# Graph layer on one core: comparison tables cut into pieces on VectorE, and two jobs moved to ScalarE

## The chip, the core and the metric

The kernel runs on one core of one Trainium2 chip. The metric is the device time of one execution in microseconds (us). Five engines work beside each other and meet only at semaphores: TensorE (PE, with its weight loads as PEld), VectorE (DVE), ScalarE (ACT), GpSimd (POOL) and SyncE (SP, which issues DMAs).

## What is computed

12,500 nodes with 256 features go through a layer norm, and then three things are added to them: a relational graph convolution over 200,000 edges of 8 types (per node and type the mean of the weighted neighbours, times that type's matrix), a linear attention with 8 heads over all nodes, and, after a second layer norm, a mixture of 6 expert networks of which the best 2 count for each node. Cut to its core:

```python
def gnn(x, src, dst, etype, ew, weight, root, bias):
    seg = etype * N + dst
    sums = segment_sum(x[src] * ew[:, None], seg)
    h = sums / maximum(segment_sum(ones, seg), 1)[:, None]        # mean by (type, dst)
    return einsum('rnc,rco->no', h.reshape(R, N, C), weight) + x @ root + bias

def mix(x):                                                       # 8 heads of 32
    q, k = elu(x @ wq + bq) + 1, elu(x @ wk + bk) + 1
    out = (q @ (k.T @ v)) / (q @ k.sum(rows) + 1e-6)              # by head
    return out @ wo + bo

def ffn(f):
    p = softmax(relu(f @ rw1 + b1) @ rw2 + b2); w, i = top_k(p, 2)
    h1 = relu(f @ e_w1[e] + e_b1[e]); h2 = relu(h1 @ e_w2[e] + e_b2[e])
    return sum over the two best e of softmax(w) * (h2 @ e_w3[e] + e_b3[e])

xn = layernorm(x)
x = x + gnn(xn, ...) + mix(xn)
return x + ffn(layernorm(x))
```

## The kernel before

**Two halves.** The first (up to about 610 us) normalizes the nodes, multiplies each by the 8 type matrices into a table `y_tab` in HBM, and builds for each edge a triple in `etab`: row of `y_tab`, target node, coefficient. The second half first makes the keys' sums of the attention (about 615 to 860 us) and then loops over 24 full super-tiles of 512 nodes (4 tiles of 128) and a last one of 2 tiles. One turn of that loop is `iteration(i, plan)`; there is one on each engine, and the engines keep step by semaphores alone. Nothing reorders instructions: each engine runs its own list as written.

**What one iteration does.** For super-tile `i` it runs the experts, and for the next one, `i+1`, it sums the edges and the attention. The edges of a super-tile come in 12 portions `p` of 6, 6 and 5 columns for each tile, a column being 128 edges. GpSimd gathers their rows from `y_tab` into `ring`. A 0/1 table of 128 edges by 128 nodes (one where the edge's target is the node) turns the sum over edges into a matmul, `aggregate(n, p)` on PE, into the PSUM tile `acc`. Portions 0 to 3 (`PLAIN`) are "weighted": VectorE writes coefficient times table into `sel` (`weighted`, L1376) and PE multiplies `ring` as it is. Portions 4 to 11 are "split": ScalarE writes the high half of coefficient times row (`high`, `row_hi`), VectorE the rest (`low_rows`, `row_lo`) and the bare 0/1 table `hot_r` (`one_hot`, L1386), one instruction for the whole portion; PE multiplies both halves.

**What a table is made of.** `iota_w` (SBUF) and `ramp` (its copy in PSUM) hold 0 to 127 along each row. `rel_w[:, n % 2, t, k]` is the target node of column `k` less the tile's first node; `tables(n)` makes it for a super-tile from the loaded triples `tab`. Comparing the one with the other gives the table.

**Where a portion is prepared and used.** With expert `e` VectorE and ScalarE prepare the portions of `SPLIT_AT[e]`, and PE sums those of `AHEAD_W3[e]`:

```python
AHEAD_W3 = {0: (3,), 1: (4,), 2: (5, 6), 3: (7, 8), 4: (9, 10), 5: (11,)}
SPLIT_AT = {0: (4,), 1: (5, 6), 2: (7, 8), 3: (9, 10), 4: (11,)}
```

So portions 5 and 6 are prepared with expert 1 and summed with expert 2, between PE's `h1` of expert 3 and its `w3` of expert 2. Portions 0 and 1 of `i+2` are prepared at the very end of iteration `i`.

**PE's banks.** Five PSUM banks are dealt out in turn to all results (`layout`), each freed by the engine that read it last. Per expert these are two results `h2(e)`, two `h1(e+1)` and two `w3(e)` (two tiles each). ScalarE and VectorE together take the hidden ones (`h_hi`, then `h_lo` on VectorE); VectorE alone takes `w3`: the instruction at L1552 adds bank times gate to `y`, twice for each bank. `queries` opens an iteration with two banks of query projections.

**The attention's denominators** (expert 1): VectorE adds epsilon, takes the reciprocal `rden` (128 x 32) and spreads it over the features into `rden_c`, which is the tile `eq` (128 x 1024); PE transposes that later (`spread`, expert 2).

## Time and profile before

| | |
|---|---|
| median of 3 runs | 2996.17 us (2993.83 to 2996.44) |
| the profiled execution | 2996.88 us, of which the span of its instructions is 2995.4 us |
| busy in the span | PE 2914.0 us (97%), VectorE 2190.0 us (73%), ScalarE 1762.9 us (59%), GpSimd 1674.2 us (56%) |
| mean granted TensorE clock | 0.991 |
| one iteration of the loop | 87.6 us (start to start of `std_c` on ScalarE: 1470.62 and 1558.22 us) |

Busy means that an instruction of the engine was in flight. An engine starts the next instruction a little before the one ahead has ended, so the time from start to start is shorter than a duration: twelve `sel` of 342 ns (median) took 3.16 us together.

### The profile page before, as it was taken

The numbers are of one execution on the slowest core, as the hardware profiler recorded it, in microseconds if no ns is written. First come the engines' busy times: TensorE is split into PE (matmuls) and PEld (weight loads), VectorE is DVE, ScalarE is ACT, GpSimd is POOL, SyncE is SP. The second block draws the span as 40 slices with busy tenths as digits, with TensorE's granted clock in tenths as the row PEclk, the third lists the DMA queues.
The fourth block names the chain that finished last, engine by engine and source line by source line (L and its number), as shares of the span: only waits on it lengthen the run. The fifth ranks groups of instructions, "written<-read, shape, count | busy, mean of one in ns | idle before, by whom it ended". The sixth has DMA issues, their size and how long they took to land.

```text
span 2995.4 us, 47258 instructions
## 1 busy us (share of the span) xinstructions
PE 2914.0 (97%) x16707; PEld 2561.0 (85%) x16708; DVE 2190.0 (73%) x5317; ACT 1762.9 (59%) x3392; POOL 1674.2 (56%) x1700
## 2 busy tenths in 40 slices
PE   7999999979989999999999999999999999999998
PEld 5887878868878888888888988888988888888887
DVE  5489564145677887777788777778887777888775
ACT  4455555524456666665666666566665666666554
POOL 1000000052267777777777777777777777777750
PEclk9999999989999999999999999999999999999999
DMA  7777777765444434444443444444344444434430
GB/s 275 272 264 274 265 275 288 293 214 199 145 130 127 128 109 133 134 130 134 122 130 106 129 130 132 133 122 126 114 134 134 134 124 130 121 121 134 134 85 11
DMA packets 181936, 471.35 MB, mean 157 GB/s; under 512 B 46902, under 2 KB 105228, under 8 KB 159715
## 3 DMA queue, kind: packets, MB, share of 16 engines
q0 software_dynamic: 80544, 221.54, 25.6%
q1 hardware_dynamic: 98960, 244.93, 22.6%
q8 instruction: 133, 2.18, 0.3%
q10 hardware_dynamic: 2196, 1.86, 0.2%
q14 instruction: 103, 0.84, 0.1%
HBM read 310.71 MB, written 158.29 MB: 157 GB/s over the span
## 4 chain that ended last, share of the span: by engine, by line
PE 63%; POOL 6%; DVE 5%; issue 3%; ACT 1%; DVEq 1%; DMA 0%; SPq 0%; ACTq 0%; POOLq 0%
PE bank L1670 41%; PE acc L1727 7%; PE acc L1733 7%; POOL ring L1150 6%; PE acc L1670 2%; DVE sel L1381 2%; PE bank L1834 1%; PE bank L1697 1%; DVE x L1480 1%; PE bank L1706 1%; PE bank L1716 1%; DVE h_lo L1510 1%; DVE stats_c L1484 1%; PE bank L1783 1%; DVEq L1482 1%
## 5 line engine op out<-in xcount | busy, mean ns | idle before, releaser
L1150 POOL DMA_INDIRECT ring<-y_tab,tab x1666 | 1657.5, 995 | 633.8 <-issue 499.7
L1224 ACT ACTIVATE h_hi<-bank,bias_t 128x512 fp32r<-128x512 f32 (+1 forms) x600 | 407.3, 679 | 302.1 <-PE bank L1670 268.5
L1510 DVE TENSOR_TENSOR h_lo<-bank,h_hi 128x512 fp32r<-128x512 f32 (+1 forms) x600 | 382.0, 674 | 229.8 <-ACT bank L1225 227.8
L778 PE MATMUL yb<-wr_hi,xhl 128*128 128x512 f32 x1568 | 498.2, 394 | 13.1 <-ACT yst L355 11.1
L1210 ACT ACTIVATE row_hi<-ring,tab 128x256 fp32r<-128x256 f32 x1091 | 451.7, 498 | 33.3 <-issue 17.7
L1401 DVE SCALAR_TENSOR_TENSOR row_lo<-ring,tab,row_hi 128x256 fp32r<-128x256 f32 x1091 | 449.4, 478 | 9.4 <-ACT row_hi L1210 9.2
L1225 ACT ACTIVATE bank<-bank,bias_t 128x512 f32<-128x512 f32 (+1 forms) x600 | 386.3, 644 | 0.0
L355 ACT ACTIVATE yst<-yb 128x512 f32<-128x512 f32 x392 | 229.3, 596 | 249.4 <-PE yb L778 219.1
L778 PEld LDWEIGHTS yb<-wr_hi,xhl 128*128 128x128 f32 x1568 | 296.2, 189 | 79.9 <-ACT yst L355 15.8
L1670 PE MATMUL bank<-ew_hi,h_hi 128*128 128x256 f32 x1176 | 343.5, 292 | 1.6 <-DVE h_lo L1510 1.4
L1670 PE MATMUL bank<-ew_lo,h_hi 128*128 128x256 f32 x1176 | 330.8, 281 | 0.0
L1670 PE MATMUL bank<-ew_hi,h_lo 128*128 128x256 f32 x1176 | 329.4, 280 | 0.0
L778 PE MATMUL yb<-wr_lo,xhl 128*128 128x512 f32 x784 | 306.9, 391 | 0.0
L1733 PE MATMUL acc<-row_hi,hot_r 128*128 128x256 f32 x1091 | 270.1, 286 | 10.7 <-DVE row_lo L1401 10.7
L1733 PE MATMUL acc<-row_lo,hot_r 128*128 128x256 f32 x1091 | 267.3, 283 | 0.0
L1727 PE MATMUL acc<-ring,sel 128*128 128x256 f32 x1150 | 264.4, 379 | 0.0
L1727 PEld LDWEIGHTS acc<-ring,sel 128*128 128x128 f32 x1150 | 214.2, 190 | 28.5
L1670 PE MATMUL bank<-h_hi,ew_hi 128*128 128x512 f32 (+1 forms) x600 | 236.7, 394 | 1.5 <-DVE h_lo L1510 1.5
L1552 DVE SCALAR_TENSOR_TENSOR y<-bank,gate,y 128x256 f32<-128x256 f32 x490 | 211.6, 477 | 35.4 <-PE bank L1670 28.9
L1670 PE MATMUL bank<-h_hi,ew_lo 128*128 128x512 f32 (+1 forms) x600 | 234.3, 390 | 0.0
L1670 PE MATMUL bank<-h_lo,ew_hi 128*128 128x512 f32 (+1 forms) x600 | 234.2, 390 | 0.0
L1670 PE MATMUL bank<-ft_hi,ew_hi 128*128 128x512 f32 (+1 forms) x600 | 232.9, 388 | 0.0
(265 smaller groups left out, 5506.6 us busy)
## 6 DMA issues: line engine op xcount, KB each, us to landing
y_tab<-yst SPq DMA_DIRECT2D x97, 1024.0 KB, 4.4
ring<-y_tab,tab POOLq DMA_INDIRECT x1666, 2.8
xt_tab<-xhl SPq DMA_DIRECT2D x25, 1024.0 KB, 4.8
xc<-xt_tab SPq DMA_DIRECT2D x25, 1024.0 KB, 5.5
xhl<-xt_tab SPq DMA_DIRECT2D x23, 1024.0 KB, 5.0
x<-x_tab SPq DMA_DIRECT2D x49, 256.0 KB, 3.1
xs<-in_x SPq DMA_DIRECT2D x24, 512.0 KB, 6.0
x_tab<-xs SPq DMA_DIRECT2D x24, 512.0 KB, 5.1
```

Source lines behind the costliest of these rows:

```text
L355: act.activation(yst[:, h, 2 * b:2 * b + 2, :], yb[(YB * u + b) % 3][:, :].rearrange("p (r n) -> p r n", r=2), ACT.Copy).then_inc(y_ev, 1)
L778: last = pe.matmul(out_ap, a, b, start=(i == 0), stop=(i == len(parts) - 1))
L1150: pool.indirect_dma_start(out=out_ap, out_offset=None, in_=y_tab[:, :], in_offset=bass.IndirectOffsetOnAxis(ap=idx_ap, axis=0)).then_inc(s ...
L1210: last = act.activation(row_hi[:, p % BUFS, q, :], ring[:, p % SLOTS, q, :], ACT.Copy, scale=tab[:, n % 2, t, k, 2:3])
L1224: act.activation(dest[:, m, 0:W], b[:, 0:W], ACT.Relu, bias=bias)
L1225: act.activation(b[:, 0:W], b[:, 0:W], ACT.Relu, bias=bias).then_inc(h_set, 1)
L1401: last = dve.scalar_tensor_tensor(out=row_lo[:, p % SLOTS, q, :], in0=ring[:, p % SLOTS, q, :], scalar=tab[:, n % 2, t, k, 2:3], in1=row_h ...
L1510: gone(dve.tensor_tensor(lo_[:, m, 0:W], bank[plan[kind, (e, m)][0]][:, 0:W], hi[:, m, 0:W].bitcast(F32), ALU.subtract))
L1552: last = dve.scalar_tensor_tensor(out=y[:, t, :], in0=b[:, (t % 2) * C:(t % 2 + 1) * C], scalar=gate[:, t, e:e + 1], in1=(y if e else x1)[ ...
L1670: last = pe.matmul(out_ap, a, b, start=(begin and i == 0), stop=(not more and i == len(parts) - 1), skip_group_check=more)
L1727: last = pe.matmul(sums(t), sel[:, p % BUFS, q, :], ring[:, p % SLOTS, q, :], start=False, stop=False, skip_group_check=True)
L1733: last = pe.matmul(sums(t), hot_r[:, p % BUFS, q, :], half, start=False, stop=False, skip_group_check=True)
```

## The change

- **Tables in pieces.** `split(n, p)` takes the place of `one_hot` and `low_rows` in the loop and in `prepare`: for each column one 128 x 128 piece of `hot_r`, then that column's `row_lo`. The wait for ScalarE's `hi_ready` stands ahead of the first piece. In an iteration the tables of a portion were made ahead of the expert's `y`; now they stand behind `y`, between the low rows. (The key stage keeps `one_hot` and `low_rows` for portions 4 to 7.)
- **`sel` from `ramp`.** `weighted` compares with `ramp` in PSUM where it read `iota_w` in SBUF.
- **`tables` on ScalarE.** Four activations for a super-tile, target node plus a bias column `neg_t` (a constant that GpSimd writes once), with expert 3; VectorE waits for `rel_set`. The first two super-tiles' are made at the head of the second half, ahead of all else on ScalarE's list.
- **The spread on ScalarE.** `by_feature` copies `rden` over the features, behind `gate_t` and ahead of the `row_hi` of portions 5 and 6; VectorE stops after the reciprocal.

```diff
+                def by_feature(i):
+                    act.wait_ge(rden_set, i + 2)
+                    act.activation(rden_c[:, :, :].rearrange("p t (h d) -> p (t h) d", h=HEADS),
+                                   rden[:, :, :].rearrange("p t h -> p (t h)").unsqueeze(2)
+                                   .to_broadcast([P, SUB * HEADS, C // HEADS]), ACT.Copy).then_inc(rden_ready, 1)
+                def tables(n):
+                    act.wait_ge(tab_in[n % 2], 16 * SUB * (n // 2 + 1))
+                    for t in range(SUB):
+                        last = act.activation(rel_w[:, n % 2, t, :], tab[:, n % 2, t, :, 1], ACT.Identity,
+                                              bias=neg_t[:, SUB * n + t:SUB * n + t + 1])
+                    last.then_inc(rel_set, 1)
...
+                        if more and e == 1:
+                            by_feature(i)
                         for p in SPLIT_AT.get(e, ()) if more else ():
                             high(i + 1, p)
+                        if more and e == EXPERTS - 3 and i + 2 < SUPER:
+                            tables(i + 2)
...
+                act.wait_ge(neg_set, 1)
+                tables(0)
+                tables(1)
...
-                    dve.reciprocal(rden[:, :, :], rden[:, :, :])
-                    dve.drain()
-                    dve.tensor_copy(rden_c[:, :, :].rearrange("p t (h d) -> p (t h) d", h=HEADS),
-                                    rden[:, :, :].rearrange("p t h -> p (t h)").unsqueeze(2)
-                                    .to_broadcast([P, SUB * HEADS, C // HEADS])).then_inc(rden_ready, 1)
+                    dve.reciprocal(rden[:, :, :], rden[:, :, :]).then_inc(rden_set, 1)
...
+                    dve.wait_ge(rel_set, n + 1)
                     tables_free(dve, n, p)
                     for q, (t, k) in enumerate(tiles_of_portion(p)):
-                        last = dve.tensor_scalar(sel[:, p % BUFS, q, :], iota_w[:, :], rel_w[:, n % 2, t, k:k + 1],
+                        last = dve.tensor_scalar(sel[:, p % BUFS, q, :], ramp[:, 0:NT], rel_w[:, n % 2, t, k:k + 1],
...
+                def split(n, p):
+                    if p >= parts(n):
+                        return
+                    tables_free(dve, n, p)
+                    if p == 0:
+                        dve.wait_ge(rel_set, n + 1)
+                    dve.wait_ge(hi_ready, split_before(n, p) + 1)
+                    for q, (t, k) in enumerate(tiles_of_portion(p)):
+                        dve.tensor_tensor(hot_r[:, p % BUFS, q:q + 1, :], ramp[:, 0:NT].unsqueeze(1).to_broadcast([P, 1, NT]),
+                                          rel_w[:, n % 2, t, k:k + 1].unsqueeze(2).to_broadcast([P, 1, NT]), ALU.is_equal)
+                        last = dve.scalar_tensor_tensor(out=row_lo[:, p % SLOTS, q, :], in0=ring[:, p % SLOTS, q, :],
+                                                        scalar=tab[:, n % 2, t, k, 2:3],
+                                                        in1=row_hi[:, p % BUFS, q, :].bitcast(F32),
+                                                        op0=ALU.mult, op1=ALU.subtract)
+                    last.then_inc(lo_ready, 1)
...
-                        for p in coming:
-                            one_hot(i + 1, p)
...
                             if h == 0 and coming:
-                                low_rows(i + 1, coming[0])
+                                split(i + 1, coming[0])
...
                         for p in coming[1:]:
-                            low_rows(i + 1, p)
-                        if more and e == EXPERTS - 3:
-                            if i + 2 < SUPER:
-                                tables(i + 2)
+                            split(i + 1, p)
```

VectorE with expert 3, where portions 9 and 10 are prepared. Before, from the hidden results' rest `h_lo` to the next expert's:

```order
L1390 TENSOR_TENSOR hot_r<-ramp,rel_w 128x768 [waits portion_used] x2
L1552 SCALAR_TENSOR_TENSOR y<-bank,gate,y 128x256 [waits items_full]
L1552 SCALAR_TENSOR_TENSOR y<-bank,gate,y 128x256
L1401 SCALAR_TENSOR_TENSOR row_lo<-ring,tab,row_hi 128x256 [waits hi_ready]
L1401 SCALAR_TENSOR_TENSOR row_lo<-ring,tab,row_hi 128x256 x5
L1372 TENSOR_SCALAR rel_w<-tab 128x17 [waits tab_in0]
L1372 TENSOR_SCALAR rel_w<-tab 128x17 x3
L1510 TENSOR_TENSOR h_lo<-bank,h_hi 128x512 [waits h_set] x4
```

The two `y` and the six `row_lo` stand there twice, once for each half of `w3`. After, the same stretch with one portion's pieces:

```order
L1578 SCALAR_TENSOR_TENSOR y<-bank,gate,y 128x256 [waits items_full]
L1578 SCALAR_TENSOR_TENSOR y<-bank,gate,y 128x256
L1429 TENSOR_TENSOR hot_r<-ramp,rel_w 128x128 [waits hi_ready,portion_used]
L1431 SCALAR_TENSOR_TENSOR row_lo<-ring,tab,row_hi 128x256
L1429 TENSOR_TENSOR hot_r<-ramp,rel_w 128x128
L1538 TENSOR_TENSOR h_lo<-bank,h_hi 128x512 [waits h_set] x4
```

The two tables of 768 columns that stood ahead of `y` have become twelve of 128 that stand behind it, each ahead of its low row, and the four `rel_w` are gone from this engine.

ScalarE with expert 1, between the gates' transpose `gate_t` and the high rows of portions 5 and 6. Before:

```order
L1250 ACTIVATE gate_t<-bank 96x512 [waits items_full]
L1210 ACTIVATE row_hi<-ring,tab 128x256 [waits portion_used,rows_in5,tab_in1]
L1210 ACTIVATE row_hi<-ring,tab 128x256 x4
L1210 ACTIVATE row_hi<-ring,tab 128x256 [waits portion_used,rows_in0,tab_in1]
L1210 ACTIVATE row_hi<-ring,tab 128x256 x5
```

After:

```order
L1266 ACTIVATE gate_t<-bank 96x512 [waits items_full]
L1205 ACTIVATE eq<-rden 128x1024 [waits rden_set]
L1226 ACTIVATE row_hi<-ring,tab 128x256 [waits portion_used,rows_in5,tab_in1]
L1226 ACTIVATE row_hi<-ring,tab 128x256 x4
L1226 ACTIVATE row_hi<-ring,tab 128x256 [waits portion_used,rows_in0,tab_in1]
```

The spread (`eq` is the tile under `rden_c`) now stands ahead of both portions' high rows.

## Rows read from the trace of the kernel before

**Rows 1.** Busy us (x instructions) by stretch: PE, PEld, DVE, ACT, POOL, clock, DMA.

```profile
1000.00:1900.00 900.00, 894.00 (x5450) 801.21 (x5449) 729.82 (x1903) 576.44 (x1095) 690.39 (x689) 1.00 0.43 126
```

**Rows 2.** Waits, PE's own: total us, times, longest.

```profile
PE bank L1670 <- DVE y L1552: 13.8, 23, 1.0
PE bank L1834 <- DVE kf_c L1584: 13.3, 5, 7.2
PE acc L1733 <- DVE row_lo L1401: 10.7, 4, 6.4
```

**Rows 3.** Timeline, VectorE, end of an iteration: start us, us, operation, xcount.

```profile
1464.09 3.16 DVE L1381 TENSOR_SCALAR sel<-iota_w,rel_w,tab 128x128 f32<-128x128 f32 x12
...
1470.68 1.66 DVE L1552 SCALAR_TENSOR_TENSOR y<-bank,gate,y 128x256 f32<-128x256 f32 x4
```

**Rows 4.** Timeline, PE, second query bank of the next iteration.

```profile
1471.61 0.72 PE L1670 MATMUL bank<-xc,wqr_hi 128*128 128x512 f32 x2 [0.57 <-DVE y L1552]
```

**Rows 5.** Groups by form, VectorE: busy us, mean ns of one, idle before.

```profile
L1401 DVE SCALAR_TENSOR_TENSOR row_lo<-ring,tab,row_hi 128x256 fp32r<-128x256 f32 x1091 | 449.4, 478 | 9.4 <-ACT row_hi L1210 9.2
...
L1552 DVE SCALAR_TENSOR_TENSOR y<-bank,gate,y 128x256 f32<-128x256 f32 x490 | 211.6, 477 | 35.4 <-PE bank L1670 28.9
L1381 DVE TENSOR_SCALAR sel<-iota_w,rel_w,tab 128x128 f32<-128x128 f32 x575 | 154.9, 356 | 78.5 <-PE acc L1727 78.4
L1390 DVE TENSOR_TENSOR hot_r<-ramp,rel_w 128x768 fp32r<-128x768 f32 x121 | 113.0, 950 | 2.2
...
L1390 DVE TENSOR_TENSOR hot_r<-ramp,rel_w 128x640 fp32r<-128x640 f32 x73 | 59.5, 815 | 0.0
...
L1495 DVE TENSOR_SCALAR xn_c<-x,mv_c,rstd_c 128x256 f32<-128x256 f32 x98 | 35.5, 422 | 2.0
...
L1359 DVE COPY eq<-rden 128x1024 f32<-128x1024 f32 x25 | 18.4, 734 | 1.8
```

**Rows 6.** Single lines, VectorE: copy into `ramp`, a table in SBUF (ns min/median/max).

```profile
L1304 DVE COPY ramp<-iota_w x1: 269/269/269, 605.9 to 605.9; 128x128 f32<-128x128 f32 x1
...
L513 DVE TENSOR_SCALAR place<-iota_w x1: 221/221/221, 175.0 to 175.0; 128x128 f32<-128x128 f32 x1
```

**Rows 7.** Groups by form, ScalarE.

```profile
L1228 ACT ACTIVATE std_c<-mv_c,eps_ln 128x4 f32<-128x4 f32 x24 | 7.1, 297 | 148.3 <-DVE mv_c L1487 148.3
...
L329 ACT ACTIVATE wr_hi<-yst 128x1024 fp32r<-128x1024 f32 x4 | 4.0, 1058 | 0.0
```

**Rows 8.** Timeline, ScalarE, expert 1 of an iteration.

```profile
1509.59 0.60 ACT L1250 ACTIVATE gate_t<-bank 96x512 fp32r<-96x512 f32 x1 [2.42 <-PE bank L1799]
1510.08 4.50 ACT L1210 ACTIVATE row_hi<-ring,tab 128x256 fp32r<-128x256 f32 x11
```

**Rows 9.** Timeline, VectorE, the same stretch.

```profile
1511.01 0.88 DVE L1552 SCALAR_TENSOR_TENSOR y<-bank,gate,y 128x256 f32<-128x256 f32 x2 [0.21 <-PE bank L1670]
1512.21 2.07 DVE L1401 SCALAR_TENSOR_TENSOR row_lo<-ring,tab,row_hi 128x256 fp32r<-128x256 f32 x5 [0.33 <-ACT row_hi L1210]
1514.20 0.87 DVE L1552 SCALAR_TENSOR_TENSOR y<-bank,gate,y 128x256 f32<-128x256 f32 x2
1515.16 1.29 DVE L1563 TENSOR_TENSOR y<-bank,y 128x512 f32<-128x512 f32 x2
1516.37 2.46 DVE L1401 SCALAR_TENSOR_TENSOR row_lo<-ring,tab,row_hi 128x256 fp32r<-128x256 f32 x6
```

**Rows 10.** Timeline, PE: first matmul of expert 3's `h1`; first of portion 6.

```profile
1515.49 0.39 PE L1670 MATMUL bank<-ft_hi,ew_hi 128*128 128x512 f32 x1
...
1519.43 0.28 PE L1733 MATMUL acc<-row_hi,hot_r 128*128 128x256 f32 x1
```

**Rows 11.** Timeline, VectorE, expert 3: first `y`, last low rows.

```profile
1534.68 0.88 DVE L1552 SCALAR_TENSOR_TENSOR y<-bank,gate,y 128x256 f32<-128x256 f32 x2
...
1538.63 2.46 DVE L1401 SCALAR_TENSOR_TENSOR row_lo<-ring,tab,row_hi 128x256 fp32r<-128x256 f32 x6
```

**Rows 12.** Timeline, PE, expert 3: last matmul of `w3`, half one; portion 10.

```profile
1534.05 0.28 PE L1670 MATMUL bank<-ew_hi,h_lo 128*128 128x256 f32 x1
...
1542.56 0.28 PE L1733 MATMUL acc<-row_hi,hot_r 128*128 128x256 f32 x1
```

More of the change, by code:

```diff
@@ L911, in gps_layer @@
             base_t = sbuf(pc, "base_t", [P, TILES_N])
+            neg_t = sbuf(pc, "neg_t", [P, TROWS])
             xtab = sbuf(pc, "xtab", [P, 3])
@@ L978, in gps_layer @@
             emptied = {"act": sem("act_emptied"), "dve": sem("dve_emptied")}
-            rden_ready, acc_full, x1_done = (sem(n) for n in ("rden_ready", "acc_full", "x1_done"))
+            rden_set, rel_set, rden_ready, acc_full, x1_done = (sem(n) for n in ("rden_set", "rel_set", "rden_ready", "acc_full", "x1_done"))
             var_c, std_c, xn_c, d_ready, ex_ready, gap_ready, g2_ready, gate_ready = (
@@ L996, in gps_layer @@
             rows_in = [sem(f"rows_in{g}") for g in range(SLOTS)]
-            xtab_in, xold_in, xrows_in, xrows_split, xsum_done, xnew_set, xnew_out, base_set, x_tab_done, xsum_free = (
+            xtab_in, xold_in, xrows_in, xrows_split, xsum_done, xnew_set, xnew_out, base_set, neg_set, x_tab_done, xsum_free = (
                 sem(n) for n in ("xtab_in", "xold_in", "xrows_in", "xrows_split", "xsum_done", "xnew_set", "xnew_out",
-                                 "base_set", "x_tab_done", "xsum_free"))
+                                 "base_set", "neg_set", "x_tab_done", "xsum_free"))
             def tiles(plan):
@@ L1143, in _ @@
                           allow_small_or_imprecise_dtypes=True).then_inc(base_set, 1)
+                pool.iota(neg_t[:, :], pattern=[[-NT, TROWS]], base=0, channel_multiplier=0,
+                          allow_small_or_imprecise_dtypes=True).then_inc(neg_set, 1)
                 def count(register):
@@ L1289, in _ @@
                         gone(act.activation(kw_sb[:, :, :], b[:, :].rearrange("p (k n) -> p k n", k=KC), ACT.Copy))
+                        by_feature(-1)
                     if p in WEIGHTS_AT:
@@ L1366, in attention @@
                         gone(dve.tensor_tensor(qf[:, k, :], qf[:, k, :], b[:, 0:NS], ALU.mult))
-                def tables(n):
-                    dve.wait_ge(tab_in[n % 2], 16 * SUB * (n // 2 + 1))
-                    for t in range(SUB):
-                        dve.tensor_scalar(rel_w[:, n % 2, t, :], tab[:, n % 2, t, :, 1], float(n * NS + t * NT), None,
-                                          ALU.subtract)
-                    dve.drain()
                 def weighted(n, p):
@@ L1411, in prepare @@
                     else:
-                        one_hot(n, p)
-                        low_rows(n, p)
+                        split(n, p)
                 def by_expert(v, n):
@@ L1596, in _ @@
                 dve.memset(zv[:, :, :, :], 1.0)
-                tables(0)
+                dve.drain()
                 for p in range(PARTS):
@@ L1627, in _ @@
                                           ALU.subtract).then_inc(w_split_c, 1)
-                tables(1)
                 prepare(1, 0)
```

## The prediction

> **What bounds the kernel now.** I read the busy time by stretch first. In the loop PE is busy 894.0 of 900 us, at full clock, while VectorE has 730 and ScalarE 576 [rows 1]. So work taken from VectorE or ScalarE buys nothing by itself. Time is won where PE waits, and lost where a later VectorE or ScalarE makes it wait. PE's own waits come next [rows 2]: in the loop one kind only, 23 times about 0.6 us for VectorE's `y`; the other two kinds belong to the key stage. The wait of 0.6 us stands at an iteration's start. VectorE runs twelve `sel`, then sums and statistics, without a pause into the four `y` [rows 3]; the second of these ends near 1471.55 us (half of 1.66 us after 1470.68), and PE's second query bank starts at 1471.61 [rows 4]. What stands in that row of VectorE is therefore paid or won one for one. Everywhere else the question is how long before PE's use VectorE is done.
>
> **Prices on VectorE.** Instructions start before the last one has ended: twelve `sel` in 3.16 us are 0.256 us from start to start, 0.09 less than the median duration of 0.342 us [rows 3]; five `row_lo` take the 1.99 us up to the next instruction, 0.398 each [rows 9]. I sum start-to-start times.
>
> *A piece of table.* 768 columns take 950 ns, 640 take 815 [rows 5]: 1.05 ns a column, 134 ns for 128. So 950 - 5 x 134 = 280 ns is a piece's duration and, less the same 0.08, 0.20 us its share. A column costs 0.20 + 0.40 = 0.60 us. A portion of 6 is 3.6 us behind `y` where it was 0.87 ahead and 2.38 behind; one of 5 is 3.0 where it was 0.73 and 1.99. Bounds: 0.13 if the fixed 0.07 is hidden beside a low row, 0.25 if alternating costs 0.05 more. I take 0.20, since both neighbours' rows give it.
>
> *`sel` from `ramp`.* No row shows this operation with PSUM as source. With two column scalars in SBUF the same operation costs (422 - 356)/128 = 0.52 ns a column, `hot_r` from `ramp` 1.05 [rows 5]. Bounds: nothing, or 128 x 0.53 = 0.07 us each. A gain is excluded as far as rows go: low rows from SBUF and `y` from PSUM take 478 and 477 ns [rows 5]. A copy of 128 x 128 into `ramp` took 269 ns, a table of that size in SBUF 221 [rows 6], which also speaks for the upper end. I take 0.07.
>
> The Trainium skill (VectorE: DVE Perf Modes, "Why PSUM operands drop a tier") says that the mode of two elements a cycle needs both read ports of SBUF, and that an fp32 operand in PSUM leaves one element a cycle. No run here shows a `sel` from PSUM. By that rule the upper end holds and the sum below stands; without it the first rival would.
>
> *Removed:* the spread (734 ns) and four small `rel_w`. The spread left a gap that VectorE spends waiting for PE at 1511.01 anyway [rows 9]; both count nothing.
>
> **ScalarE.** The spread is one activation of 128 x 1024; one of that size took 1058 ns [rows 7], 0.95 from start to start. Its wait is met: `rden` is ready before `gate_t`. What is queued behind it is `row_hi` of portions 5 and 6 [rows 8], and VectorE already waits 0.33 us for portion 5's [rows 9]. The four `rel_w` (297 ns for a small one with a bias column [rows 7], some 0.2 each) come with expert 3; all 0.8 us of them would only delay hidden results that VectorE reads behind portion 10's pieces, and their waiter, `sel`, comes two experts later. GpSimd's extra constant and the DMAs are off the path: no transfer is added.
>
> **The sum for one iteration,** place by place.
>
> 1. *End of the iteration.* 12 x 0.07 = 0.8 us more ahead of `y`, on the path already [rows 3, 4]: **+0.8**.
> 2. *Expert 1, bank.* Portion 5's high rows end 0.95 later, so the pieces start at 1513.17 and take 3.0: the second pair of `y` starts at 1516.16 where it started at 1514.20 [rows 9], and ends near 1517.04. PE needs that bank for expert 3's `h1`, which started at 1515.49 [rows 10]: **+1.6**.
> 3. *Portion 6.* Behind the `y` come 1.2 us of bias adds and 3.6 us of pieces: ready at about 1522.0. PE wanted it at 1519.43 [rows 10], now 1.6 later: 1521.0, **+1.0**.
> 4. *Portion 10.* With no tables ahead of it, VectorE's first `y` moves up to the end of PE's first half of `w3`, about 1534.4 [rows 12], instead of 1534.68 [rows 11]. Two pairs of `y` (0.8 each) and two portions (3.6 each) end at 1543.2; before it was 1541.1 [rows 11]. PE wants portion 10 at 1542.56 [rows 12]: **+0.7**.
>
> Portions 7 and 8 end about 1.2 later, portion 11 1.0; by the same sums they just arrive in time, and portion 4 easily does. Together 4.1 us. There are 23 iterations that prepare all 12 portions and a `sel` pair: 94 us. The 24th has expert 1's bank: 1.6. The head: about 17 `sel` of portions 1 to 3 and twelve ahead of the loop (29 x 0.07 = 2), VectorE's last four split portions back to back with the spread ahead of a `row_hi` (0.3 each and 0.95), and ScalarE's key work behind the loading of the second table (about 1.5): some 6, bounds 0 and 10. Sum: +101 us. The profiled execution took 2996.88 us with a span of 2995.4, so it lies 0.7 above the median, and the new time is 2996.9 + 101 = **3098 us**.
>
> **Rivals.**
>
> *First: `sel` costs the same from `ramp`.* For it: no row shows otherwise directly. Against it: the slopes [rows 5] and the copy into PSUM [rows 6]. Place 1 falls away (24 x 0.8 = 19) and 1 of the head: 3078 us.
>
> *Second: part of a piece is hidden.* The fixed 0.07 runs beside the low row, a column costs 0.53. Place 2 gives 1.3, place 3 0.6, place 4 none, place 1 stays: 2.7 x 23 + 1.3 + 5 = 68, thus 3065 us. Against it: no pair of operations in the rows overlaps more than 0.09.
>
> *Third: pieces dearer.* At 0.25 a piece places 2 to 4 are 1.9, 1.3 and 1.4, and portion 8 comes late by some 0.3: 5.7 x 23 + 9 = 140, thus 3137 us. For it: two more waits at the head of a portion, and operations change at every step.
>
> *Fourth, the other side: reading `ramp` runs beside reading SBUF.* A piece is then free beside its low row (a column 0.40), and `sel` falls to its 0.134 us of columns. VectorE would do the tables for nothing, place 1 turns to a gain of the whole 0.77 us that PE now loses there (24 x 0.77 = 18), places 3 and 4 vanish, and place 2 keeps 0.6 from the spread. That is -0.2 x 23 + 2 = about -3: 2994 us. It decides from a column of about 0.43 us and a `sel` under 0.19. Against it: `y`, which reads PSUM, and `row_lo` follow each other in the rows without any gain.
>
> **How the numbers follow.** Forecast 0.60, first rival 0.15, second 0.10, third 0.06, fourth 0.05, and 0.04 for a gain that I don't see. 0.2% (6 us) is about what a measurement of this kernel can tell from no change. The fourth lies within that, the unseen gain beyond it: faster 0.04, same 0.05, slower 0.91. The range reaches down past the second rival and its uncertain head to 3050, and up to the head's bound and pieces of 0.22, 3118; it leaves out the third, the fourth and the unseen gain, and some tails.
>
> **What would show it.** In the profile after: `hot_r` 1091 times at about 280 ns; `sel` at 410 ns instead of 342; an iteration of 91.7 us instead of 87.6; PE's wait for `y` at the query banks at 1.4 us; new waits of PE for `row_lo`, two in an iteration, and at expert 3's `h1` one for `y` of about 1.5; VectorE waiting 1.3 us for ScalarE's `row_hi` with expert 1. If the iteration is still 87.6 us, VectorE's prices are wrong; if `sel` stays at 342, the first rival holds; if `h1` doesn't wait with expert 1, the spread's place is.

## The result, and the profile after

The changed kernel takes 3107.82 us (median of 4 runs, 3106.42 to 3110.3) where the kernel before took 2995.0 us beside it (median of 4 runs, 2991.61 to 2996.44): 1.0379 times as long, 95% interval 1.0361 to 1.0397. That is 112.8 us more; the prediction was 101 more. The profiled executions differ by as much: a span of 3107.6 us against 2995.4.

Where the 112.2 us of span lie can be read from ScalarE's `std_c`, the square root that opens every turn of the loop. Its first instance starts at 869.28 us instead of 860.37: the head costs 8.9. From there to the last instance it is 103.6 us more, and the tail is 0.2 shorter. Two neighbours in the timeline of ScalarE after (start us, duration us, engine, line, operation; in brackets the idle time before it and who ended it):

```profile
1511.53 0.30 ACT L1244 ACTIVATE std_c<-mv_c,eps_ln 128x4 f32<-128x4 f32 x1 [6.61 <-DVE mv_c L1515]
...
1603.58 0.30 ACT L1244 ACTIVATE std_c<-mv_c,eps_ln 128x4 f32<-128x4 f32 x1 [6.61 <-DVE mv_c L1515]
```

A turn takes 92.05 us here and 92.02 in the middle of all, instead of 87.60: 4.42 more. The stretch of [rows 1] after, with the same columns:

```profile
1000.00:1900.00 900.00, 860.39 (x5178) 762.66 (x5178) 716.20 (x2114) 561.08 (x1086) 639.00 (x666) 1.00 0.41 122
```

PE's clock is at its upper level (1.00) as before, but PE is busy 860 of 900 us instead of 894: the time went into PE's waits, not into slower work of PE. VectorE is busy less than before (716 instead of 730) although it has 211 more instructions in these 900 us: fewer turns fit into them, and in each VectorE idles longer for PE, which waits for VectorE. The waits of PE in the whole execution, which answer [rows 2] (total us, times, longest us):

```profile
PE bank L1692 <- DVE y L1578: 65.0, 47, 1.4
PE acc L1755 <- DVE row_lo L1431: 38.8, 49, 6.7
PE bank L1856 <- DVE kf_c L1607: 20.1, 9, 12.5
```

The first kind had 23 waits, now 47: a second one in each turn. The second kind had 4, now 49: two new ones in each turn. The longest of the third, in the key stage, grew from 7.2 to 12.5 us; it belongs to the head.

The groups of VectorE by form, for [rows 5] (count | busy us, mean ns of one | idle before and its releaser):

```profile
L1431 DVE SCALAR_TENSOR_TENSOR row_lo<-ring,tab,row_hi 128x256 fp32r<-128x256 f32 x1068 | 506.7, 474 | 0.0
...
L1429 DVE TENSOR_TENSOR hot_r<-ramp,rel_w 128x128 fp32r<-128x128 f32 x1068 | 301.3, 282 | 35.7 <-ACT row_hi L1226 35.7
...
L1394 DVE TENSOR_SCALAR sel<-ramp,rel_w,tab 128x128 f32<-128x128 f32 x575 | 190.0, 402 | 81.9 <-PE acc L1749 81.9
```

A piece takes 282 ns and a `sel` from PSUM 402. There are 1068 pieces and not the 1091 that the prediction gave: the key stage keeps whole tables for portions 4 to 7, which are 23 columns. On ScalarE the spread takes 1044 ns and a small `rel_w` 303 (for [rows 7]):

```profile
L1205 ACT ACTIVATE eq<-rden 128x1024 f32<-128x1024 f32 x25 | 26.1, 1044 | 4.7 <-DVE rden L1381 4.7
L1212 ACT ACTIVATE rel_w<-tab,neg_t 128x17 f32<-128x17 f32 x100 | 23.2, 303 | 5.3 <-DMA tab<-etab 5.3
```

**The four places in one turn.** The second query bank on PE (for [rows 4]), and the row of VectorE ahead of it (for [rows 3]):

```profile
1512.52 0.74 PE L1692 MATMUL bank<-xc,wqr_hi 128*128 128x512 f32 x2 [1.32 <-DVE y L1578]
```

```profile
1504.26 3.91 DVE L1394 TENSOR_SCALAR sel<-ramp,rel_w,tab 128x128 f32<-128x128 f32 x12
...
1511.59 1.66 DVE L1578 SCALAR_TENSOR_TENSOR y<-bank,gate,y 128x256 f32<-128x256 f32 x4
```

Twelve `sel` take 3.91 us instead of 3.16, and PE's gap grows from 0.57 to 1.32 us: 0.75 and 0.75, one for one.

Expert 1 on ScalarE and VectorE (for [rows 8, 9]; of portion 5's five pairs the first and the last stand here):

```profile
1550.56 0.60 ACT L1266 ACTIVATE gate_t<-bank 96x512 fp32r<-96x512 f32 x1 [2.42 <-PE bank L1821]
1551.05 1.04 ACT L1205 ACTIVATE eq<-rden 128x1024 f32<-128x1024 f32 x1
1552.00 4.50 ACT L1226 ACTIVATE row_hi<-ring,tab 128x256 fp32r<-128x256 f32 x11
```

```profile
1554.20 0.29 DVE L1429 TENSOR_TENSOR hot_r<-ramp,rel_w 128x128 fp32r<-128x128 f32 x1 [1.34 <-ACT row_hi L1226]
1554.41 0.47 DVE L1431 SCALAR_TENSOR_TENSOR row_lo<-ring,tab,row_hi 128x256 fp32r<-128x256 f32 x1
...
1556.78 0.47 DVE L1431 SCALAR_TENSOR_TENSOR row_lo<-ring,tab,row_hi 128x256 fp32r<-128x256 f32 x1
1557.17 0.87 DVE L1578 SCALAR_TENSOR_TENSOR y<-bank,gate,y 128x256 f32<-128x256 f32 x2
```

From the first piece to the `y` behind the portion it is 2.97 us for 5 columns, 0.59 each. VectorE waits 1.34 us for ScalarE, which has the spread ahead of its `row_hi`. PE's three waits that follow from it and from the pieces, at `h1` of expert 3, at portion 6 and at portion 10 (for [rows 10, 12]):

```profile
1558.10 0.50 PE L1692 MATMUL bank<-ft_hi,ew_hi 128*128 128x512 f32 x1 [1.43 <-DVE y L1578]
1558.43 0.40 PE L1692 MATMUL bank<-ft_lo,ew_hi 128*128 128x512 f32 x1
1558.66 0.39 PE L1692 MATMUL bank<-ft_hi,ew_lo 128*128 128x512 f32 x1
...
1563.04 0.39 PE L1755 MATMUL acc<-row_hi,hot_r 128*128 128x256 f32 x1 [0.75 <-DVE row_lo L1431]
...
1587.07 0.39 PE L1755 MATMUL acc<-row_hi,hot_r 128*128 128x256 f32 x1 [0.46 <-DVE row_lo L1431]
```

The idle time in brackets is not the whole price: the matmul ahead of a gap counts as busy a little longer. I therefore compared PE's matmuls of one turn one by one in the two traces, by the time from start to start (the seventh turn; the rows above are of the eighth, where portion 6 waits 0.91 instead of 0.87). A second price comes out by this: the matmul behind a wait takes 0.10 us longer until the next one starts. It is in the rows above: 1558.10 to 1558.43 is 0.33 us, 1558.43 to 1558.66 0.23.

| place | predicted more | the wait is longer by | and the matmul behind it |
|---|---|---|---|
| query banks | 0.8 | 0.75 | none new |
| `h1` of expert 3 | 1.6 | 1.60 | 0.11 |
| portion 6 | 1.0 | 0.87 | 0.10 |
| portion 8 | 0 | 0.03 | 0.10 |
| portion 10 | 0.7 | 0.62 | 0.10 |
| spread thinly over the rest | 0 | 0.1 | |

### The profile page after: what moved, and what is told of

The parts are those of the page before. It is cut to its first block, busy times and chain, and to the rows that moved or that the text cites. A ratio compares the mean times of both kernels' runs of the same rounds, so it can differ in the third digit from the quotient of the medians.

```text
span 3107.6 us, 48377 instructions
## 1 busy us (share of the span) xinstructions
PE 2939.9 (95%) x16707; PEld 2564.3 (83%) x16708; DVE 2246.6 (72%) x6070; ACT 1807.4 (58%) x3517; POOL 1627.4 (52%) x1701
## 4 chain that ended last, share of the span: by engine, by line
PE 54%; DVE 18%; ACT 4%; issue 3%; DVEq 2%; DMA 0%; SPq 0%; ACTq 0%
PE bank L1692 32%; PE acc L1749 8%; DVE row_lo L1431 6%; PE acc L1755 6%; DVE hot_r L1429 4%; DVE sel L1394 3%; PE acc L1692 2%; DVE y L1578 2%; ACT row_hi L1226 2%; PE bank L1719 1%; PE bank L1856 1%; DVE x L1508 1%; ACT eq L1205 1%; PE bank L1738 1%; PE bank L1728 1%
## 5 line engine op out<-in xcount | busy, mean ns | idle before, releaser
L1153 POOL DMA_INDIRECT ring<-y_tab,tab x1666 | 1610.5, 967 | 776.7 <-issue 490.8
L1431 DVE SCALAR_TENSOR_TENSOR row_lo<-ring,tab,row_hi 128x256 fp32r<-128x256 f32 x1068 | 506.7, 474 | 0.0
L1429 DVE TENSOR_TENSOR hot_r<-ramp,rel_w 128x128 fp32r<-128x128 f32 x1068 | 301.3, 282 | 35.7 <-ACT row_hi L1226 35.7
L1755 PE MATMUL acc<-row_hi,hot_r 128*128 128x256 f32 x1091 | 279.3, 292 | 40.9 <-DVE row_lo L1431 38.8
L1755 PEld LDWEIGHTS acc<-row_hi,hot_r 128*128 128x128 f32 x1091 | 207.5, 190 | 59.3 <-DVE row_lo L1431 52.4
L1394 DVE TENSOR_SCALAR sel<-ramp,rel_w,tab 128x128 f32<-128x128 f32 x575 | 190.0, 402 | 81.9 <-PE acc L1749 81.9
```

Source lines behind the costliest of these rows:

```text
L1153: pool.indirect_dma_start(out=out_ap, out_offset=None, in_=y_tab[:, :], in_offset=bass.IndirectOffsetOnAxis(ap=idx_ap, axis=0)).then_inc(s ...
L1394: last = dve.tensor_scalar(sel[:, p % BUFS, q, :], ramp[:, 0:NT], rel_w[:, n % 2, t, k:k + 1], tab[:, n % 2, t, k, 2:3], ALU.is_equal, ALU ...
L1429: dve.tensor_tensor(hot_r[:, p % BUFS, q:q + 1, :], ramp[:, 0:NT].unsqueeze(1).to_broadcast([P, 1, NT]), rel_w[:, n % 2, t, k:k + 1].unsqu ...
L1431: last = dve.scalar_tensor_tensor(out=row_lo[:, p % SLOTS, q, :], in0=ring[:, p % SLOTS, q, :], scalar=tab[:, n % 2, t, k, 2:3], in1=row_h ...
L1755: last = pe.matmul(sums(t), hot_r[:, p % BUFS, q, :], half, start=False, stop=False, skip_group_check=True)
```

## The experiments

Two questions were left. Do the four parts cost what the sum says when each stands alone, or is a share of the 112.8 us made by their meeting? And what makes the pieces dear: their number, or the place behind `y` that came with them? Each ratio below is to the kernel before; a turn is read from `std_c` start to start and is the median.

| kernel | ratio to before (95% interval) | one turn, us |
|---|---|---|
| before | | 87.60 |
| changed | 1.0379 (1.0361 to 1.0397) | 92.02 |
| `sel` from `ramp`, alone | 1.0061 (1.0047 to 1.0074) | 88.34 |
| spread on ScalarE, alone | 1.0058 (1.0044 to 1.0072) | 88.28 |
| pieces behind `y`, alone | 1.0238 (1.0225 to 1.0252) | 90.62 |
| `rel_w` on ScalarE, alone | 1.0022 (1.0011 to 1.0032) | 87.73 |
| whole tables behind `y` | 1.0124 (1.0108 to 1.0139) | 89.12 |
| pieces ahead of `y` | 1.0043 (1.0030 to 1.0057) | 87.75 to 89.4 |
| changed, spread back on VectorE | 1.0292 (1.0276 to 1.0309) | 91.13 |
| half of the `sel` behind `y` | 0.9938 (0.9924 to 0.9951) | 86.73 |
| changed, second `rel_w` late | 1.0373 (1.0359 to 1.0387) | 92.02 |

### `sel` from `ramp` alone

```diff
-                        last = dve.tensor_scalar(sel[:, p % BUFS, q, :], iota_w[:, :], rel_w[:, n % 2, t, k:k + 1],
+                        last = dve.tensor_scalar(sel[:, p % BUFS, q, :], ramp[:, 0:NT], rel_w[:, n % 2, t, k:k + 1],
```

> The kernel before, with one edit: the twelve sel of an iteration's end read ramp in PSUM. Theory (each place of the loop loses its own amount, worked out in the prediction): a sel is 60 ns longer, as in the changed kernel (402 instead of 342 ns), all twelve stand ahead of y, so PE's wait at the query banks grows by 12 x 0.06 = 0.73 us; iteration 88.3 instead of 87.6 us, nothing else in the loop waits; about +19 us in all. Rival (the sel is dear only beside other late work of VectorE, and alone its 0.7 us has cover): iteration 87.6, +0 to +2 us.

Measured: 1.0061 times the time before, 18 us more; a turn 88.34 us, 0.74 more. The whole difference stands at the query banks: PE's second bank starts 0.74 us later there, every other matmul keeps its distance. The median `sel` takes 401 ns instead of 342. The theory holds; the rival, that 0.7 us alone would be covered, falls.

### The spread alone

```diff
+                        if more and e == 1:
+                            by_feature(i)
                         for p in SPLIT_AT.get(e, ()) if more else ():
                             high(i + 1, p)
...
-                    dve.reciprocal(rden[:, :, :], rden[:, :, :])
-                    dve.drain()
-                    dve.tensor_copy(rden_c[:, :, :].rearrange("p t (h d) -> p (t h) d", h=HEADS),
-                                    rden[:, :, :].rearrange("p t h -> p (t h)").unsqueeze(2)
-                                    .to_broadcast([P, SUB * HEADS, C // HEADS])).then_inc(rden_ready, 1)
+                    dve.reciprocal(rden[:, :, :], rden[:, :, :]).then_inc(rden_set, 1)
```

> The kernel before, with one edit: ScalarE spreads the reciprocals over the features, ahead of the row_hi of portions 5 and 6. Theory: the row_hi end 0.95 us later, VectorE's y at expert 1 as well, and PE had 0.35 us to spare there (of 1.95 us of delay 1.6 showed in the changed kernel): PE waits 0.6 us at the first bank of h1 of expert 3, iteration 88.2, and about 2 us at the head; +16 us. Rival one (VectorE has lost its own 0.7 us of spreading, so that the exchange is even): 0 per iteration, 0 to +2 us. Rival two (ScalarE's 0.95 us counts in full): +0.95 per iteration, +24 us.

Measured: 1.0058, 17 us; a turn 88.28; the first `std_c` comes at 864.03 us, 3.7 later, where I had 2 (the same edit stands once in the head, `by_feature(-1)`). PE waits 0.58 us at `h1` of expert 3, and the matmul behind it takes 0.11 more. So VectorE's own 0.7 us that it is rid of buys nothing (rival one falls), and PE has 0.37 us to spare at that place (rival two falls): the theory's number.

### The pieces alone

```diff
-                        one_hot(n, p)
-                        low_rows(n, p)
+                        split(n, p)
...
-                        for p in coming:
-                            one_hot(i + 1, p)
...
-                                low_rows(i + 1, coming[0])
+                                split(i + 1, coming[0])
...
-                            low_rows(i + 1, p)
+                            split(i + 1, p)
```

> The kernel before, with one edit: the bare tables in pieces of 128, between the low rows, behind y. Theory: PE's wait at h1 of expert 3 is 0.6 us (3.0 us of portion 5 behind the first pair of y where 2.0 stood, less 0.35 to spare), for portion 6 about 1.0, for portion 10 about 0.7, and the query banks stay at 0.77; iteration 90.0 to 90.1, about +57 us. Rival (the waits of the changed kernel come from the spread on ScalarE, which pushes the same work): portion 6 waits less than 0.3, iteration below 89.

Measured: 1.0238, 71 us, more than the 57 expected; a turn 90.62, 3.0 more. PE's waits in 1000 to 2900 us, some 21 turns (total us, times, longest):

```profile
PE acc L1744 <- DVE row_lo L1416: 25.0, 41, 1.1
PE bank L1681 <- DVE y L1563: 24.4, 42, 0.9
```

The second row is the two places of `y`: the query banks, which wait as before, and `h1` of expert 3. Matmul by matmul a turn gains 0.73 at `h1` of expert 3, 0.90 at portion 6, 0.65 at portion 10, 0.05 at portion 8, 0.21 at the first matmul of expert 4's `w3` behind portion 10, and 0.10 behind each of these five waits. The fifth is a wait for the low half of expert 4's hidden results, `h_lo`. VectorE, then PE:

```profile
1565.96 0.45 DVE L1372 TENSOR_SCALAR rel_w<-tab 128x17 f32<-128x17 f32 x4
1566.48 2.48 DVE L1523 TENSOR_TENSOR h_lo<-bank,h_hi 128x512 fp32r<-128x512 f32 x4
```

```profile
1567.82 0.39 PE L1681 MATMUL bank<-ew_hi,h_hi 128*128 128x256 f32 x1
```

The second of the four `h_lo` is the one that this matmul needs, and the four `rel_w` push it back by 0.52 us. It is not a wait for expert 3's `y`, as the expectation of a later run below has it: that `y` had ended at 1562.48. The three expected waits have their sizes; what I had left out are the 0.5 us behind the waits and the late `h_lo`. The rival (the spread pushes portion 6) falls: portion 6 waits as long without the spread.

### `rel_w` on ScalarE alone

```diff
+                        if more and e == EXPERTS - 3 and i + 2 < SUPER:
+                            tables(i + 2)
...
+                act.wait_ge(neg_set, 1)
+                tables(0)
+                tables(1)
...
-                        if more and e == EXPERTS - 3:
-                            if i + 2 < SUPER:
-                                tables(i + 2)
```

> The kernel before, with one edit: ScalarE makes rel_w. Theory: nothing in the loop (iteration 87.6), since their waiter, sel, comes two experts later; at the head the key features begin 2.9 us later, because ScalarE waits for the second super-tile's triples before it loads its second function table: +3 us. Rival one (the hidden results behind the four small activations are late): up to +0.8 per iteration, +20 us. Rival two (VectorE, which is rid of four small operations and a drain, gains it back): 0 or below.

Measured: 1.0022 (1.0011 to 1.0032), 7 us; a turn 87.73 instead of 87.60. The first `std_c` starts at 866.21 us, 5.8 after the one before, and the rest is 0.13 us a turn. In the turn that I compared matmul by matmul none is more than 0.012 us further from its neighbour than before; the 0.13 us is spread over many. Neither rival holds, and the theory had the head too cheap (3 us). What spreads the 0.13 stays open. But the like of it, 0.1 to 0.2 us a turn in no one place, is in every trace with `rel_w` on ScalarE and in none without, so it belongs to this part. The 5.8 us at the head are less sure than they look: the run with half of the `sel` behind `y`, whose head is that of the kernel before, has its first `std_c` 2.1 us later than it (862.47), so differences of single heads are uncertain by about 2 us.

### Number or place: whole tables behind `y`

```diff
+                def split(n, p):
+                    if p >= parts(n):
+                        return
+                    dve.wait_ge(hi_ready, split_before(n, p) + 1)
+                    one_hot(n, p)
+                    low_rows(n, p)
...
-                        for p in coming:
-                            one_hot(i + 1, p)
...
-                                low_rows(i + 1, coming[0])
+                                split(i + 1, coming[0])
...
-                            low_rows(i + 1, p)
+                            split(i + 1, p)
```

> The kernel before, with one edit: the bare table of a portion stays one instruction, but stands behind the first pair of y and behind the wait for row_hi, where the pieces stand. This separates place from number. Theory (both count; the place decides that anything counts): a portion of 5 is 2.7 us behind y instead of 3.0 in pieces and 2.0 before, one of 6 is 3.25; so PE waits 0.45 at h1 of expert 3, 0.55 for portion 6, next to nothing for portion 10, each with 0.1 for starting again; iteration 88.8 to 88.9, about +30 us. Rival one (only the number of instructions costs): 87.6, +0. Rival two (only the place costs, and a piece is as cheap as its share of a whole table): as with pieces, 90.6, +70 us.

Measured: 1.0124, 37 us; a turn 89.12, 1.5 more. The waits: 0.36 at `h1` of expert 3, 0.56 at portion 6, next to none at portion 10, 0.15 for the late `h_lo` of expert 4 behind portion 10, and 0.10 behind each. Neither extreme holds: the place alone, with the same number of instructions as before, makes half of what the pieces cost.

### Number or place: pieces ahead of `y`

```diff
-                    (t, k), size = tiles_of_portion(p)[0], len(tiles_of_portion(p))
-                    dve.tensor_tensor(hot_r[:, p % BUFS, 0:size, :], ramp[:, 0:NT].unsqueeze(1).to_broadcast([P, size, NT]),
-                                      rel_w[:, n % 2, t, k:k + size].unsqueeze(2).to_broadcast([P, size, NT]), ALU.is_equal)
+                    for q, (t, k) in enumerate(tiles_of_portion(p)):
+                        dve.tensor_tensor(hot_r[:, p % BUFS, q:q + 1, :], ramp[:, 0:NT].unsqueeze(1).to_broadcast([P, 1, NT]),
+                                          rel_w[:, n % 2, t, k:k + 1].unsqueeze(2).to_broadcast([P, 1, NT]), ALU.is_equal)
```

> The kernel before, with one edit: the bare tables in pieces, but all of a step's pieces at the place of the whole tables, ahead of y and of the wait for row_hi. Theory: two portions take 11 x 0.20 = 2.2 us instead of 1.6; the 0.6 us more fall into time in which VectorE waits there for PE's w3 (0.9) or ScalarE's row_hi (0.33); iteration 87.6 to 87.9, at most +6 us. Rival (a piece costs its 0.07 wherever it stands, 62 pieces are 4.3 us less what 8 whole tables had fixed): +1.7 us an iteration or more, +40 us.

Measured: 1.0043, 13 us. Most early turns take 87.75 us, 0.15 more, as the theory has it: the same number of pieces costs next to nothing where VectorE waits anyway. (The 0.15 is the wait for expert 4's `h_lo` behind portion 10 again: 0.05, and 0.10 behind it.) The rival (+1.7 a turn) falls. But later turns take 87.8 to 89.4 us, which no theory had. In four of them VectorE waits, up to 1.3 us, for ScalarE's `row_hi` of portion 10; one of these:

```profile
1545.33 2.46 DVE L1401 SCALAR_TENSOR_TENSOR row_lo<-ring,tab,row_hi 128x256 fp32r<-128x256 f32 x6 [1.29 <-ACT row_hi L1210]
```

and ScalarE itself had stood 4.3 us for something that the trace doesn't name:

```profile
1542.77 2.52 ACT L1210 ACTIVATE row_hi<-ring,tab 128x256 fp32r<-128x256 f32 x6 [4.32 <-issue]
```

Such waits of ScalarE without a releaser come to 55.7 us (18 waits) in 1000 to 2900 us here and to 17.7 (12 waits) before. They are waits for late gathers. The trace also keeps when each DMA landed: in all 30 cases the `row_hi` starts 0.07 us after the last landing for the portion's slot of `ring` (1542.70 us in the row above). GpSimd has no time to spare for them: it starts a column's gather 1.25 us after the one before (median), never pauses for more than 0.6 us between 1000 and 2800 us, and the 68 columns of a turn are 85 us of 87.6. In the first seven turns here it gathers some 66 columns a turn, uses up its lead, and from then on ScalarE waits for it in every turn. Why its lead ends earlier here than in the kernel before stays open.

Together the two runs answer the question: number alone 0.15 us a turn (3.5 of the 10.3 us that the loop loses in the run with pieces ahead of `y`; the rest lies in its turns with late gathers), place alone 1.5, both 3.0. The fixed part of a piece costs only where there is no more slack to cover it, and the place took the slack.

The Trainium skill (Perfetto Trace Analysis, "Optimizing Scalar/DVE Operations") advises: "If Scalar/Vector aren't saturated, but are causing bubbles on other engines, breaking up instructions may allow work to be completed sooner." VectorE is that engine here (busy 81% in [rows 1], the releaser of PE's only wait of the loop), but the table wasn't the instruction that the bubble waited for, and no run here shows a gain: broken up in its place it costs 0.4%, late gathers included, broken up and moved 2.4%.

### The changed kernel with the spread back on VectorE

```diff
-                        if more and e == 1:
-                            by_feature(i)
...
-                    dve.reciprocal(rden[:, :, :], rden[:, :, :]).then_inc(rden_set, 1)
+                    dve.reciprocal(rden[:, :, :], rden[:, :, :])
+                    dve.drain()
+                    dve.tensor_copy(rden_c[:, :, :].rearrange("p t (h d) -> p (t h) d", h=HEADS),
+                                    rden[:, :, :].rearrange("p t h -> p (t h)").unsqueeze(2)
+                                    .to_broadcast([P, SUB * HEADS, C // HEADS])).then_inc(rden_ready, 1)
```

> The changed kernel, with one part undone: VectorE spreads the reciprocals again, behind the reciprocal. Theory: PE's wait at h1 of expert 3 falls from 1.60 to the 0.74 that the pieces alone gave, the other waits stay, and the wait for expert 3's y that the pieces alone showed behind portion 10 (0.2) does not come back, since VectorE no longer makes rel_w there; iteration 91.15 instead of 92.02; at the head VectorE no longer waits 3.2 us for ScalarE; about -23 us against the changed kernel, 3085 us. Rival one (the spread costs what it cost alone, 0.66): 91.35, 3091 us. Rival two (the whole 1.6 is the spread's): 90.4, 3069 us.

Measured: 3082.11 us (3079.46 to 3086.93), 26 less than changed; a turn 91.13. PE's wait at `h1` of expert 3 is 0.69, portions 6 and 10 wait 0.90 and 0.63, about as in the changed kernel, and the wait behind portion 10 (for expert 4's `h_lo`) is not there. So beside the pieces the spread costs 0.89 us a turn, and alone 0.68: the 0.37 us that PE has to spare at that place is eaten by whichever part comes first. Neither rival holds (91.35 and 90.4 us a turn). The opposite happens behind portion 10: the 0.31 us that the pieces alone lost at expert 4's `h_lo` is gone once VectorE no longer makes `rel_w` between that portion and the `h_lo`. That is the only gain that a part of this change brings in the runs.

Parts alone add up: 18 + 17 + 71 + 7 = 113 us, against 112.8 for all of them. Per turn 0.74 + 0.68 + 3.02 + 0.13 is 4.57 against 4.42; the two interactions, about +0.2 and -0.3, nearly cancel.

### Half of the `sel` behind `y`

```diff
                         if e == EXPERTS - 1 and i + 2 < SUPER:
                             prepare(i + 2, 0)
-                            prepare(i + 2, 1)
...
                         if e == EXPERTS - 1:
                             dve.drain()
                             dve.sem_inc(y_ready, 1)
+                            if i + 2 < SUPER:
+                                prepare(i + 2, 1)
```

> The kernel before, with one edit: of the twelve sel at an iteration's end the second six (portion 1) stand behind the last expert's y. Theory: y starts 1.5 us earlier, PE's wait of 0.77 at the query banks goes, and nothing takes its place, since the scales that now come behind six sel start when they did before; iteration 86.85 instead of 87.60; -17 us, 2979 us. Rival (the normalization behind the six sel becomes late): iteration unchanged or longer, 0 to +20 us.

Measured: 2976.17 us (2975.28 to 2980.16), ratio 0.9938 (0.9924 to 0.9951): 19 us faster than the kernel before, the fastest version of this study; a turn 86.73. It takes place 1 of the prediction the other way: 1.5 us less ahead of `y` win the 0.74 us that PE lost there and the 0.11 behind it. In 1000 to 1900 us PE is now busy without a gap:

```profile
1000.00:1900.00 900.00, 900.00 (x5506) 810.05 (x5505) 737.92 (x1924) 579.00 (x1099) 687.92 (x697) 1.00 0.43 127
```

The rival falls: the scales behind the six `sel` are not late. ScalarE now waits for late gathers in 16 turns (32.7 us in 1000 to 2900 us), so GpSimd is what this version runs into next.

### The head: the second super-tile's `rel_w` later

```diff
                 act.wait_ge(neg_set, 1)
                 tables(0)
-                tables(1)
...
                         act.activation(w_hi[j][:, :, :, :], stage[j % 2][:, :, :, :], ACT.Copy).then_inc(w_hi_set, 1)
+                tables(1)
                 for s in range(SUPER - 1):
```

> The changed kernel, with one move: at the head of the second half ScalarE makes only the first super-tile's rel_w; the second super-tile's comes at the end of the head, behind the last weights and ahead of the loop. Theory: ScalarE no longer waits 5.3 us for the second super-tile's triples ahead of its function table, the key features begin at about 621.5 us instead of 624.06, PE's longest wait there falls from 12.5 to about 9, and the key stage, in which PE is busy 95%, passes that on: first std_c of the loop 2 to 3 us earlier, loop unchanged at 92.02; about 3105 us instead of 3107.8. Rival (what the wait cost is made up for in the key stage): first std_c at 869 as before, no change in time.

Measured: 3105.92 us (3103.32 to 3108.13), ratio 1.0373 (1.0359 to 1.0387); by time alone this can't be told from the changed kernel's 3107.8. The profile tells it: the first key features start at 620.13 us instead of 624.06, the first `std_c` at 864.99 instead of 869.28, a turn stays 92.02. What ScalarE did in the changed kernel at that point:

```profile
614.80 0.92 ACT L1212 ACTIVATE rel_w<-tab,neg_t 128x17 f32<-128x17 f32 x4
621.06 0.94 ACT L1212 ACTIVATE rel_w<-tab,neg_t 128x17 f32<-128x17 f32 x4 [5.33 <-DMA tab<-etab]
622.01 1.28 ACT L1290 ACT_TABLE_LOAD   x1
623.31 0.42 ACT L1290 ACTIVATE ek_c<-zv 128x256 f32<-128x256 f32 x1
```

It waits 5.33 us for a DMA whose result VectorE first needs for the `sel` at 861.63 us, and the whole key stage stands behind it. By the profiles moving it wins back 3.9 us at the key features and 4.3 of the head's 8.9 at the first `std_c`; the medians differ by 1.9.

## Why the prediction held, step by step

**What bounds the kernel: right.** PE's waits carry all but 0.1 us of a turn's loss; the clock stays, and what VectorE and ScalarE were relieved of shows in no turn except for the 0.3 us behind portion 10.

**Prices: right.** A piece 282 ns (predicted 280), a column with its low row 0.59 us (0.60), the spread 1044 ns (1058 from its nearest row). A `sel` went up by 60 ns where I took 70, so place 1 is 0.75 instead of 0.8. This decides against the first rival, as the runs with `sel` alone and `sel` behind `y` do. The Trainium skill (VectorE: DVE Perf Modes, "Why PSUM operands drop a tier") has an fp32 operand in PSUM cost the mode of two elements a cycle; 402 against 342 ns for 128 columns agrees with it in its direction. The second rival (a piece partly hidden), the third (0.25 a piece) and the fourth (reads of PSUM free beside reads of SBUF) fall with the 0.59 us a column.

**Place 2: right to the tenth.** 1.60 us predicted and measured. The runs told its two sources apart: alone the spread makes PE wait 0.58 there and the pieces 0.73.

**Portions 6 and 10: right in place, 0.1 too high each** (0.87 and 0.62 for 1.0 and 0.7; the working for portion 10 itself gives 0.64, from 1543.2 less 1542.56). That the other portions "just arrive in time" held for 4, 7 and 11; portion 8 is late by 0.03, which is enough to pay the 0.10 behind a wait. One hand-over was not looked at and came out well by luck: expert 4's `h_lo` behind portion 10. The pieces alone make PE wait there, and only the removal of `rel_w`, which I had counted as nothing, keeps that 0.31 us out of the sum.

**The term that was missing** is that 0.10 us: a wait of PE costs more than its length. Four new waits with it are 0.41 us a turn, 9.4 us in 23 turns. My four places at 23 turns, with 1.6 for the 24th (it lost 2.1), made 95.6 us; the loop lost 103.6. The places alone, 3.87 us as measured, would have made 91.

**The head: right within its bounds (0 to 10), 3 too low at the value taken.** That it came so near is in part luck. I gave 1.5 us to ScalarE's key work for standing behind the second super-tile's `rel_w`; it is about 4, most of it ScalarE's wait for the triples. I gave the spread 0.95 ahead of a `row_hi`; with the spread back on VectorE the first `std_c` of the changed kernel comes 3.9 us earlier (865.37). Against that, the 2 us for `sel` and the 1.2 for the pieces don't show: alone, their first `std_c` come 0.2 us later and 0.4 earlier than before. At the spread the two engines wait for each other in turn. ScalarE, then VectorE, then PE after:

```profile
854.30 1.06 ACT L1205 ACTIVATE eq<-rden 128x1024 f32<-128x1024 f32 x1 [4.66 <-DVE rden L1381]
```

```profile
857.45 0.29 DVE L1429 TENSOR_TENSOR hot_r<-ramp,rel_w 128x128 fp32r<-128x128 f32 x1 [3.19 <-ACT row_hi L1226]
```

```profile
860.57 0.39 PE L1755 MATMUL acc<-row_hi,hot_r 128*128 128x256 f32 x1 [2.15 <-DVE row_lo L1431]
```

ScalarE holds the next `row_hi` back behind a spread that waits for VectorE's reciprocal; VectorE gets to that reciprocal only behind a whole portion, and then stands 3.19 us for the `row_hi`. The lesson is that a step moved to another engine's list takes its wait along for everything queued behind it. In the loop the same wait was met, as predicted, and cost nothing.

The sum came out 11 us low in 112: too much by 0.05 to 0.13 us at three places, too little by the price behind the waits (9.4 us), the head (3) and the thin 0.1 a turn. These are all sizes; no step of the mechanism failed.

## What to carry to other kernels

When an engine is full, work taken from its neighbours buys nothing, and each neighbour has only a fixed slack at each place where the full engine picks up its results: look up that slack before moving or cutting anything, and count every new wait at its length plus the restart. Cutting an instruction costs its fixed part only where no slack is left, but moving it from ahead of a hand-over to behind it can use up that slack by itself. The one wait that the profile of before showed in the loop was worth 0.6%, and it went by moving six instructions past the hand-over, without taking work from any engine.

## What was not expected of the hardware

- **The matmul behind a wait.** After every wait of PE for VectorE the first matmul takes 0.10 us longer until the next can start: 0.33 instead of 0.23 us for 512 columns and 0.22 instead of 0.12 for 256, at `h1` of expert 3, at the query banks and at each portion, in all runs that have the wait, even where the wait itself is 0.03 us.
- **The clock after a long wait at the head.** The stretches 850 to 855, 855 to 860 and 860 to 865 us, before and then after, with the columns of [rows 1]; the granted clock is the third number from the right:

```profile
850.00:855.00 5.00, 5.00 (x31) 4.84 (x31) 4.92 (x17) 0.00 (x0) 3.85 (x4) 0.77 0.38 105
855.00:860.00 5.00, 5.00 (x24) 4.22 (x23) 4.74 (x15) 0.00 (x0) 3.82 (x4) 1.00 0.52 127
860.00:865.00 5.00, 5.00 (x36) 4.74 (x35) 3.26 (x11) 3.97 (x6) 3.79 (x4) 1.00 0.38 107
```

```profile
850.00:855.00 5.00, 1.23 (x5) 1.23 (x6) 4.17 (x15) 0.70 (x1) 3.83 (x4) 0.50 0.61 184
855.00:860.00 5.00, 3.41 (x16) 3.01 (x15) 2.55 (x9) 3.63 (x7) 3.79 (x4) 0.66 0.36 107
860.00:865.00 5.00, 4.43 (x18) 3.81 (x19) 5.00 (x15) 0.00 (x0) 3.79 (x4) 0.68 0.40 110
```

  In both kernels PE stood over 6 us for portion 10's low rows and then worked at the lower level (0.50, which is 1.2 GHz). Before, it worked on without a gap and was back at 1.00 (2.4 GHz) by 855 us. After, the second wait of 2.15 us came in between: the clock was back at 1.00 from 858.4 us, as that wait began, and fell to 0.50 again from 861.8 to 865.2, while PE worked. The run with the second `rel_w` late has the same wait and the same second fall; the run with the spread alone, which waits 1.10 us there, has no second fall. So at the head a wait went with a loss of clock beside its own length; in the loop, with its shorter waits, the clock stayed at 1.00.
